# Ten one-hot tables, a four-chunk z, transposes between the products, and ids spread twice by TensorE in a DLRM top tower

## The reference

```python
e = jnp.stack([tbl_0[ids[:, 0]], ..., tbl_25[ids[:, 25]]], axis=1)      # 512 x 26 x 128
combined = jnp.concatenate([dense[:, None, :], e], axis=1)              # 512 x 27 x 128
interactions = jnp.einsum('bfd,bgd->bfg', combined, combined)
z = jnp.concatenate([dense, interactions[:, iu, ju]], axis=1)           # pairs i < j
h = jnp.concatenate([z, dense], axis=1)                                 # 512 x 607
h = jnp.maximum(h @ W_top1 + b_top1, 0.0)                               # 512 x 512
h = jnp.maximum(h @ W_top2 + b_top2, 0.0)                               # 512 x 256
y = h @ W_top3                                                          # 512 x 1
```

## Time and profile before

| | us |
|---|---|
| three timed runs | 150.27, 152.44, 154.34 (median 152.44) |
| span of the profiled execution, first to last instruction | 152.9 |
| PE busy, PEld busy | 115.3 (75%), 95.1 (62%) |
| DVE, ACT busy | 51.1 (33%), 49.8 (33%) |
| POOL busy | 83.9 (55%) |
| first product matmul (L511) starts | 55.98 |
| last scores copied (L401) | 151.05 to 151.33 |

### The profile page before, as it was taken

The page is one execution under the profiler, slowest core; times in us unless marked ns, Lnnn a source line. Parts: engine busy times, 40 slices in busy tenths (PEclk is TensorE's granted clock), DMA queues, the critical chain, the costliest instruction groups (busy, mean ns, idle before and its releaser), DMA issues.

```text
span 152.9 us, 3980 instructions
## 1 busy us (share of the span) xinstructions
PE 115.3 (75%) x1789; PEld 95.1 (62%) x1789; DVE 51.1 (33%) x88; ACT 49.8 (33%) x98; POOL 83.9 (55%) x91
## 2 busy tenths in 40 slices
PE   0339401999379965599899899958999949995993
PEld 0127201677157654486788788647989739994691
DVE  6665600076457810712103800234500405104100
ACT  5045203368499840703000800204500106104011
POOL 4777777777787877777777777777710000000000
PEclk9999955569978999557999999997799996999659
DMA  1684447999644322221222221122210000000000
GB/s 43 151 192 164 166 164 227 270 248 238 172 166 167 119 53 57 50 57 51 55 53 56 58 51 51 51 56 56 60 30 0 0 9 0 4 4 0 4 0 1
DMA packets 5547, 12.82 MB, mean 84 GB/s; under 512 B 2025, under 2 KB 3049, under 8 KB 5277
## 3 DMA queue, kind: packets, MB, share of 16 engines
q0 software_dynamic: 2688, 5.51, 15.2%
q1 hardware_dynamic: 2832, 7.05, 15.0%
q10 hardware_dynamic: 10, 0.01, 0.0%
HBM read 12.56 MB, written 0.00 MB: 82 GB/s over the span
## 4 chain that ended last, share of the span: by engine, by line
PE 57%; DMA 25%; DVE 7%; issue 7%; ACT 2%; SPq 1%; ACTq 0%
DMA table_sb<-tbl 25%; PE h_ps L539 17%; PE gram_ps L511 9%; PE h_ps L563 7%; PE h_ps L534 6%; PE fill_ps L485 5%; DVE zT L391 5%; PE gram_ps L462 3%; PE gram_ps L539 3%; PE gram_ps L464 3%; DVE featT L385 2%; ACT featT L301 1%; PE gram_ps L534 1%; PE h_ps L573 1%; DVE h L396 1%
## 5 line engine op out<-in xcount | busy, mean ns | idle before, releaser
L289 POOL DMA_INDIRECT gathered<-tbl,ids_sb x84 | 83.1, 989 | 26.9 <-issue 25.3
L539 PE MATMUL h_ps<-zT,w_inter_sb 122*128 122x128 f32 (+1 forms) x196 | 29.2, 295 | 1.6 <-DVE zT L391 1.6
L539 PEld LDWEIGHTS h_ps<-zT,w_inter_sb 122*128 122x128 f32 (+1 forms) x196 | 27.3, 203 | 4.7 <-DVE zT L391 1.9
L462 PE MATMUL gram_ps<-onehot,table_hi 125*128 125x512 f32 x40 | 20.8, 519 | 4.8 <-DVE table_lo L424 4.7
L314 ACT ACTIVATE zT<-gram_ps 26x224 f32<-26x224 f32 (+4 forms) x40 | 12.1, 302 | 37.7 <-PE gram_ps L511 36.9
L418 DVE TENSOR_TENSOR onehot<-h_ps,rowno 125x1536 fp32r<-125x1536 f32 x10 | 17.5, 1755 | 17.8 <-PE gram_ps L464 16.9
L511 PE MATMUL gram_ps<-featT 128*26 128x26 f32 (+2 forms) x1280 | 15.5, 188 | 9.0 <-issue 5.8
L391 DVE COPY zT<-gram_ps 26x224 f32<-26x224 f32 (+4 forms) x40 | 12.9, 323 | 24.6 <-PE gram_ps L511 23.5
L511 PEld LDWEIGHTS gram_ps<-featT 128*26 128x26 f32 (+1 forms) x1280 | 13.2, 102 | 11.9 <-issue 7.5
L464 PE MATMUL gram_ps<-onehot,table_lo 125*128 125x512 f32 x40 | 19.6, 490 | 0.0
L307 ACT ACTIVATE featT<-fill_ps 128x512 f32<-128x512 f32 (+1 forms) x14 | 9.1, 656 | 26.4 <-PE fill_ps L485 26.4
(11 more groups left out here) (33 smaller groups left out, 55.5 us busy)
## 6 DMA issues: line engine op xcount, KB each, us to landing
table_sb<-tbl SPq DMA_DIRECT2D x5, 500.0 KB
w_inter_sb<-w_inter SPq DMA_DIRECT2D x1, 1792.0 KB, 29.9
gathered<-tbl,ids_sb POOLq DMA_INDIRECT x84, 3.8
oh_ids_sb<-oh_ids SPq DMA_DIRECT2D x1, 1000.0 KB
w_dense_sb<-w_dense SPq DMA_DIRECT2D x1, 512.0 KB, 25.0
w_sb<-w SPq DMA_DIRECT2D x1, 512.0 KB, 26.8
dense_sb<-dense SPq DMA_DIRECT2D x1, 256.0 KB, 23.2
oh_ids_sb<-oh_ids SPq DMA_DIRECT2D x1, 250.0 KB
```

The costliest lines, as they stand in the source:

```text
L289: pool.indirect_dma_start(out=gathered[:, t, pos - GATHERED[0], :], out_offset=None, in_=tables[table], in_offset=bass.IndirectOffsetOnAxi ...
L462: nc.tensor.matmul(lookup_ps(k), table_hi[:, k % 2, rows], onehot[:, c, :], start=(c == 0), stop=False)
L539: last = nc.tensor.matmul(layer1_ps(t, n), w_inter_sb[0:k, c, units], zT[0:k, c, tile], start=False, stop=(c == CHUNKS - 1), skip_group_ch ...
```

## The change

`ONEHOT_TABLES` grows from 5 to 10 tables, so 16 gathers and four full transpose groups a tile are left instead of 21 and six. One-hot tables are padded to 1024 rows, which makes 128 partitions. One-hot matrices get two buffers, hi and lo parts three; gathered rows go from four tile buffers to three. The broadcast DMAs go: `spread_ids` now runs two matmuls, one into `h1_ps` for DVE and one into `h2_ps` for ACT. DVE compares six chunks in one instruction. Lookup results are copied to `featT` two tables at a time. A row of `featT` has 32 slots; slots 27 to 31 repeat the dense vector and four others (`COPIED`). All 32 slots are multiplied by 27, and `zT` has 4 chunks of 128 rows: each 32-row quadrant is written twice, first whole with the columns `BELOW`, then over its first `CUT` rows with the columns `ABOVE`. That is 16 copies an engine and tile. The zeroing of `zT` goes. The dense features get their own contiguous `denseT` for layer 1. Layer 3 runs once for three tiles and once for the last. The order on PE, DVE and ACT is written out anew.

```diff
-ONEHOT_TABLES = (0, 1, 3, 6, 8)
...
+ONEHOT_TABLES = (0, 1, 3, 6, 8, 11, 12, 14, 15, 16)
 ONEHOTS = len(ONEHOT_TABLES)
 ROWS = 1000
 RCHUNKS = 8
-RPARTS = ROWS // RCHUNKS
+PADDED = P * RCHUNKS
+RAW_BUFS = 3
+ROW_BUFS = 3
+SPLIT_BUFS = 3
...
+SLOTS = 32
+DENSE_SLOT = 2
+PAIR_SLOTS = ((4, 7), (9, 10), (0, 1), (3, 5), (6, 8))
+COPIED = (2, 4, 7, 9, 10)
+FIRST_GATHERED = 1 + ONEHOTS
+GROUP = 4
+GROUPS = [range(p, p + GROUP) for p in range(FIRST_GATHERED, FEATS, GROUP)]
...
+ZCHUNKS = 4
+CUT = (3, 9, 16, 22)
+ABOVE = ((0, 6, 7, 13), (3, 5, 8, 10), (11, 12, 15, 16), (14, 17, 18, 21))
+BELOW = ((13, 19, 20, 26), (22, 23, 24, 25), (0, 1, 3, 4), (5, 6, 8, 9))
+ZCOPIES = 2 * len(CUT)
+
+AFTER_LOOKUP = [[], [(0, 0)], [(0, 1)], [(0, 2)], [(0, 3)], [(1, 0)], [(1, 1)], [], [], []]
...
+        def lookup_pair(pair):
+            return gram_ps[pair % 2][:, :].rearrange("d (f b) -> d b f", f=2)
+
+        def pair_target(pair, slots):
+            return featT[:, :, slots[0]:slots[1] + 1:slots[1] - slots[0]]
...
-            sp.dma_start(oh_ids_sb[:, 0, :], oh_ids[0].partition_broadcast(RPARTS)).then_inc(oh_ids_in[0], 16)
             load_table(1)
-            sp.dma_start(oh_ids_sb[:, 1:, :], oh_ids[1:].partition_broadcast(RPARTS)).then_inc(oh_ids_in[1], 16)
-            sp.dma_start(dense_sb[:, :, :], dense.rearrange("(t p) d -> p t d", p=P)).then_inc(dense_in, 16)
+            sp.dma_start(dense_sb[:, :, :], dense).then_inc(dense_in, 16)
             for k in range(2, ONEHOTS):
                 load_table(k)
-            sp.dma_start(w_dense_sb[:, :, :], w_dense).then_inc(w_dense_in, 16)
+                if k == 5:
+                    sp.dma_start(w_dense_sb[:, :, :], w_dense).then_inc(w_dense_in, 16)
+                    sp.dma_start(small_sb[:, :], small).then_inc(small_in, 16)
             sp.dma_start(w_inter_sb[:, :, :], w_inter).then_inc(w_inter_in, 16)
...
+            def pair_to_featT(pair):
+                act.wait_ge(lookup_done, 2 * (pair + 1))
+                if PAIR_SLOTS[pair][0] in COPIED:
+                    copy = FEATS + COPIED.index(PAIR_SLOTS[pair][0])
+                    nc.scalar.activation(pair_target(pair, (copy, copy + 1)), lookup_pair(pair), ACT.Copy) \
+                        .then_inc(copied, 1)
+                nc.scalar.activation(pair_target(pair, PAIR_SLOTS[pair]), lookup_pair(pair), ACT.Copy) \
+                    .then_inc(lookup_read, 2)
...
+            def products_to_zT(t, half):
+                j = 2 + half
+                act.wait_ge(gram_ready, t + 1)
+                for q in range(4):
+                    nc.scalar.activation(z_target(t, j, q, QUAD), z_source(t, j, BELOW[q], QUAD), ACT.Copy) \
+                        .then_inc(z_act, 1)
+                for q in range(4):
+                    act.wait_ge(z_act, ZCOPIES * (2 * t + half) + q + 1)
+                    nc.scalar.activation(z_target(t, j, q, CUT[q]), z_source(t, j, ABOVE[q], CUT[q]), ACT.Copy) \
+                        .then_inc(z_act, 1)
...
-                act.wait_ge(oh_ids_in[min(k, 1)], 16)
+                act.wait_ge(ids_for_act, k + 1)
+                if k >= 2:
+                    act.wait_ge(lookup_done, k - 1)
                 for c in range(DVE_CHUNKS, RCHUNKS):
-                    done = k * (RCHUNKS - DVE_CHUNKS) + c - DVE_CHUNKS
-                    if done:
-                        act.wait_ge(onehot_act, done)
-                    nc.scalar.activation(id_off[:, :], oh_ids_sb[:, k, :], ACT.Abs,
+                    nc.scalar.activation(onehot[:, k % 2, c, :], h2_ps[:, :], ACT.Abs,
                                          bias=minus_rowno[:, c:c + 1]).then_inc(id_off_ready, 1)
-                    if k > 0:
-                        act.wait_ge(onehot_used, RCHUNKS * (k - 1) + c + 1)
-                    act.wait_ge(id_off_ready, done + 1)
-                    nc.scalar.activation(onehot[:, c, :], id_off[:, :], ACT.Relu, bias=1.0, scale=-1.0) \
-                        .then_inc(onehot_act, 1)
+                act.wait_ge(id_off_ready, (RCHUNKS - DVE_CHUNKS) * (k + 1))
+                nc.scalar.activation(onehot[:, k % 2, DVE_CHUNKS:, :], onehot[:, k % 2, DVE_CHUNKS:, :].bitcast(fp32), ACT.Relu,
+                                     bias=1.0, scale=-1.0).then_inc(onehot_act, RCHUNKS - DVE_CHUNKS)
                 if k + 1 < ONEHOTS:
                     high_parts(k + 1)
                 if k == 1:
                     act.wait_ge(filled[0], 1)
-                    nc.scalar.activation(featT[:, :, 0], fill_ps[0][:, :], ACT.Copy).then_inc(fill_read[0], 1)
+                    nc.scalar.activation(denseT[:, :], fill_ps[0][:, :], ACT.Copy).then_inc(denseT_ready, 1)
+                    nc.scalar.activation(featT[:, :, FEATS], fill_ps[0][:, :], ACT.Copy).then_inc(copied, 1)
+                    nc.scalar.activation(featT[:, :, DENSE_SLOT], fill_ps[0][:, :], ACT.Copy).then_inc(fill_read[0], 1)
+                if k >= 2 and k % 2 == 0:
+                    pair_to_featT(k // 2 - 1)
                 if k >= 1:
...
+            last_slots = PAIR_SLOTS[-1]
+            act.wait_ge(lookup_done, ONEHOTS - 1)
+            nc.scalar.activation(featT[:, :, last_slots[0]], lookup_ps(ONEHOTS - 2), ACT.Copy).then_inc(last_pair_read, 1)
+            act.wait_ge(lookup_done, ONEHOTS)
+            for batch in (slice(0, P), slice(P, BATCH)):
+                nc.scalar.activation(featT[:, batch, last_slots[1]], lookup_ps(ONEHOTS - 1)[:, batch], ACT.Copy) \
+                    .then_inc(last_pair_read, 1)
...
+                dve.wait_ge(ids_for_dve, k + 1)
+                if k >= 2:
+                    dve.wait_ge(lookup_done, k - 1)
+                if k == 0:
+                    compare(0, 0, DVE_CHUNKS // 2)
+                    low_parts(0)
+                    compare(0, DVE_CHUNKS // 2, DVE_CHUNKS)
+                else:
+                    compare(k, 0, DVE_CHUNKS)
+                    low_parts(k)
...
             def spread_ids(k):
 
                 if k == 0:
                     pe.wait_ge(row_pick_ready, 1)
                     pe.wait_ge(oh_rows_ready, 1)
-                if k >= 2:
-                    pe.wait_ge(onehot_dve, DVE_CHUNKS * (k - 1))
-                nc.tensor.matmul(oh_ids_ps(k), row_pick[:, k, :], oh_ids_r[:, :], start=True, stop=True) \
-                    .then_inc(ids_psum, 1)
+                else:
+                    pe.wait_ge(onehot_dve, DVE_CHUNKS * k)
+                nc.tensor.matmul(h1_ps[:, :], row_pick[:, k, :], oh_ids_r[:, :], start=True, stop=True) \
+                    .then_inc(ids_for_dve, 1)
+                if k > 0:
+                    pe.wait_ge(id_off_ready, (RCHUNKS - DVE_CHUNKS) * k)
+                nc.tensor.matmul(h2_ps[:, :], row_pick[:, k, :], oh_ids_r[:, :], start=True, stop=True) \
+                    .then_inc(ids_for_act, 1)
...
-                            gram_ps[stage % 2][QUAD * j:QUAD * j + rows, col + first:col + rows],
-                            featT[:, b, 0:rows], featT[:, b, 1 + first:1 + rows], start=True, stop=True)
-                if part == N1 - 1:
+                        b = t * P + j * QUAD + s
+                        last = nc.tensor.matmul(product_ps(t)[QUAD * j:QUAD * (j + 1), SLOTS * s:SLOTS * s + FEATS],
+                                                featT[:, b, :], featT[:, b, 0:FEATS], start=True, stop=True)
...
+                for n in range(N1):
+                    nc.tensor.matmul(layer1_ps(t, n), w_dense_sb[:, 0, n * P:(n + 1) * P], denseT[:, t * P:(t + 1) * P],
+                                     start=(n == 0 or (t == LAST and n == N1 // 2)), stop=False, skip_group_check=True)
...
+            products(0, 0)
+            fill(1, 2)
+            products(0, 1)
+            fill(1, 3)
+            products(0, 2)
+            fill(2, 0)
+            products(0, 3)
```

477 lines of the change are left out of this document (234 added, 243 removed).

## The result

The changed kernel takes 124.42 us (median of six runs, 122.70 to 125.86), the kernel before beside it 152.94 (150.27 to 154.34): a ratio of 0.813, 95% interval 0.802 to 0.823. Head and tail moved in the directions forecast, and both came out shorter than forecast. Three of the six runs took 122.70 to 123.48 us at a mean granted clock of 0.986 to 1.000 and three 125.36 to 125.86 at 0.972; the profiled execution is the slowest of them, 125.86.

The account below looks back on a forecast made before the run. Before, table loads and waits for ids bound the head, PE the tail; afterwards ACT was to set the head. Head 67, tail 65.2, score copy 0.3 and way to memory 1.6 gave 134 us, range 126 to 144.

Parts of the forecast that it names:

- ACT is the fullest and decides the length.: Head: ACT's chain of copies, ids and high parts sets the length, 62 us, putting the first product at 67.
- The pair copies: Head, ACT: six copies of two tables' lookups to featT at 1.6 us each, bounds 1.2 and 2.2, 9.6 in all.
- The ids: Head, ACT: ids of eight tables at 2.5 us, 20.0; 34 gaps of 0.03 and short waits add 2.0.
- over 50 was named as a sign of being right: Head: ACT busy over 50 us there would show the forecast right.
- PE's round was put at 4.5 us: Head, PE: per table 18 matmuls of 512 columns at 0.23 and half a group of transposes, 4.5 us, ten times 45.
- The loads at nothing: Head: table loads cost no time, since three buffers give each a table round of 5 us and ACT hides them.
- products and stops: Tail, PE: 16 product parts at 0.87 us, 13.9; two mid-run stops, read as instruction fetches, 3.8.
- The first rival: Tail bound by fetching instructions: four or five more stops, each with half clock behind, +10, 144 us; chance 0.12.
- Layer 1, dense, layers 2 and 3, transposes: Tail, PE: 64 chunk matmuls 16.1 us, 16 contiguous dense ones 4.0, layer 2 8.1, layer 3 2.0, transposes 5.4.
- Waits 8.6 and half clock 3.3: Tail, PE: waits on z copies, middle stretches and last activation, 8.6 us; layer 2 slowed twice by the clock, 3.3.
- The fourth rival: Whole kernel cheaper than priced: pair copies at 1.2, no half clock, few stops, 125 us; chance 0.10.
- GpSimd at nothing: Gathers: 64 instead of 84 end near 85 us, last rows needed near 100, so POOL costs nothing.

Follow-up runs that it names:

- the kernel with both changes: Changed kernel with ScalarE's ids by broadcast DMA, no second spread, and the last transpose groups one place earlier: 123.49 us, ratio 0.810 to the kernel before.
- the second profile of the changed kernel: Changed kernel, unchanged, run again on a chip with pauses in the head: 173.36 us, kernel before 227.1; tail 60.18 us.

## Why the prediction was off, step by step

**The step that failed: "ACT is the fullest and decides the length."** Forecast 62 us for ACT's chain and 67 for the first product. Measured: ACT's chain ends at 55.96, PE's rounds decide, and the first product comes at 61.42. Against the span of 124.0 the forecast is 10.1 us too long: 5.6 in the head, 4.5 in the tail. Two terms made ACT's chain too long.
- The pair copies were put at 1.6 us; five of six took 1.07 to 1.12, one 1.97: 7.5 us (5.3 + 2.2 in the groups) instead of 9.6. I chose the middle of two bounds where the lower one was right for nearly all. The forecast also misread the copies' slots: by `COPIED` the extra pairs go to (28, 29) and (30, 31), since 27 is the dense vector's, and not to (27, 28). By the Trainium skill's rule on lines of 16 bytes, which the forecast named, only (3, 5) then lies in two. With five copies at the lower bound and one at the upper, 8.2, the rule would have been nearer than my middle.
- The ids were put at 2.5 a table, and 34 gaps of 0.03 with short waits added 2.0. In a row ACT's instructions overlap: L318 starts at 30.21 and takes 1.06, L302 starts at 31.18, 0.09 earlier than that ends. Two L315 and one L318 take 2.3 together. The Trainium skill, "ScalarE: Activation LUTs", section on what ACT_TABLE_LOAD costs, says that back-to-back ACTIVATEs overlap by about 93 ns; by that, the trace agrees, and the gaps should have been subtracted rather than added. The 2.0 was about met all the same, by waits for PE of 2.2 (0.86, 0.81 and 0.55).

From start to start, ACT's chain from the dense copies (17.46) to the last relu's end (55.96) is: dense copies 2.3 (forecast 3.0), ids of eight tables 18.5 (20.0), high parts 7.0 (7.4), pair copies 6.7 (9.6), group copies 1.7 (2.1), waits 2.2 (2.0).

ACT's busy time in the head is 46.8 us, where over 50 was named as a sign of being right. It ends its last relu at 55.96, makes one copy, and then waits 3.3 us for PE's lookup. PE's round was put at 4.5 us; it is 4.97, since half a group of transposes is a whole group in six of ten rounds and the first matmul of a run takes 0.42 rather than 0.23. Ten rounds, the first at half clock and the last three without transposes, are the head from 10.3 us on. The forecast's own PE round, nine times behind its 18, would have given about 59; with 4.97 in the six rounds that have transposes it comes near the 61.42. That ACT is not the bound is shown by the kernel without slot copies (no gain), and that PE's matmuls are by the round of 4.73 without the second spread. DVE stands just behind: its 48 us of work were forecast rightly (48.3), and with the second spread gone it is full.

**The loads at nothing: right.** One wait of 1.7 us for the first table is left of 12.6, and a table lands 4.1 us after its issue (median). The padding did it, alone worth 12 us in the old kernel. That the broadcasts are gone mattered little: in the kernel with both changes 2.6 MB of them are back, over 128 partitions, and ACT waits 1.3 us for a table and 1.2 for ids, once each. The rule on 125 and 128 partitions of the Trainium skill, "DMA: Bandwidth & Descriptors", that the forecast named, agrees with the 239 against 172 GB/s.

**The tail: products and stops.** Products 12.6 us (13.9), within the bounds: a part shows 0.75 where one of the narrower 26 by 26 shows 0.77, and from start to start they are 0.68 and 0.70, so the added columns cost nothing. Stops 5.4 (3.8): tile 0 has two of them, 2.6 us in all, where one of 1.9 was put, tile 1 one of 0.57, the last tile one of 2.25. The first rival, four or five more stops of about 2 us, did not come. The stop in the last tile's run shrinks when other work stands in between. That the stops are instruction fetches, as the forecast read them, no run shows.

**Layer 1, dense, layers 2 and 3, transposes: right in size.** 16.6 with one block at half clock (16.1), 4.1 (4.0), 9.3 with one at half clock (8.1 + 1.65), 2.0 (2.0), 5.3 (5.4). Four chunks for seven are shown to be worth 9.7, where the forecast had 12. The 7 us that it gave to the dense matmuls are not borne out as the price of the step: the step costs PE 3.2.

**Waits 8.6 and half clock 3.3: too much, and counted twice.** The named waits are 5.3: 1.30 behind tile 0, 0.59 behind the last tile, 0.66, 0.80, 0.80 and 0.45 between, 0.71 for the last activation. I took 2.0 us of wait behind the last tile *and* a spell at half clock ahead of it. Both fill the same time, until the z copies end: 3.52 + 0.59 in one profile, 1.89 + 2.22 in the other, with the dense matmuls between. The clock was not free elsewhere: from 74.30 to 79.50 us the profile has a granted clock of 0.67, and the two chunk blocks and two parts there take 5.20 us where such blocks and parts take 1.09 and 0.69 at full clock, about 1.6 us more. In the second profile of the changed kernel on the chips with pauses it fell behind the last wait and cost 1.5. So the tail's 4.5 us are waits 3.3 too much (1.4 of them behind the last tile, where the slow layer 2 had filled the time), layers 1 and 2 with their clock 1.6 too much (27.5 forecast, 25.9 measured) and products 1.3 too much, less stops 1.6 too little.

The fourth rival, "cheaper than priced" with 125 and a chance of 0.10, has the number right and most of its terms wrong, which is luck: the pair copies did take 1.1, but the engine that makes them did not decide; half clock came, and the stops were 5.4 us and not few.

**GpSimd at nothing: right, with a margin of about 15 us** (last gather at 85.33, its transposes at 101.8), which 20 gathers use up.

## What to carry to other kernels

When two limits end at the same event, only one of them may stand in the sum: a slow clock ahead of a wait is paid out of the wait, and one behind it is paid in full. For each engine of a pipelined loop add up one round with its real first-instruction and overlap figures from the rows, and compare the rounds before saying which engine decides; here PE 4.97, DVE 4.8 (48.3 over ten) and ACT 4.7 (46.8 over ten) were too near to call from rounded terms. Removing work from ACT (the slot copies) changed nothing, and removing 0.23 from PE gave back 0.19 before DVE was full. Where an edit thins one queue (GpSimd's), test what the rest of the change is worth with that queue as full as before.

## What the runs showed of the hardware

- A copy of 1024 float32 by ACT in pairs of slots takes 1.07 to 1.12 us, about as much as one contiguous instruction of that size (L302, 1.04; L318, 1.06), even with slots 4 and 7, but with slots 3 and 5 it costs 1.97, and that follows the slots. The Trainium skill, "SBUF — State Buffer", section on door 1, says that SBUF works in lines of 16 bytes and each crossing costs; by that, (3, 5) alone of the six lies in two lines, and the trace agrees.
- A moving operand with a step of 32 elements doubled a float32 matmul of 128 columns, 0.44 for 0.22 us (84.09 and 87.01 in the rows above).
- The granted clock stands at 1.00 in the window of the first lookup, where its matmuls take 0.43 us each. In the kernel before, matmuls of 0.43 us lie in a stretch, 44.0 to 46.8 us, with a clock of 0.50. At the start of an execution the matmuls' distance is the better witness. The window of the changed kernel:

```profile
10.30:16.00 5.70, 5.70 (x15) 4.44 (x15) 4.22 (x2) 3.27 (x4) 4.48 (x5) 1.00 0.29 76
```

- Padding five tables and their ids from 125 to 128 partitions adds bytes and still shortens the way: 239 GB/s for 172 in the head, and the first product 19.2 us earlier.
- On three of five chips both kernels took 1.4 to 1.5 times as long, with pauses in the head in which one engine waited up to 44 us. The profiles do not explain them. The cause stays open.
